# Delta rule layer: the convolution's input is copied from PSUM to SBUF by ScalarE before VectorE reads it

## The chip, the cores and the metric

The kernel runs on one core of a Trainium2 chip. The time is the device time of one execution in microseconds (us); of several runs the median counts.

## What is computed

The reference is two layers of two blocks each. The change is in the first block alone, a gated delta rule over 8 sequences of 512 tokens with 128 channels, 8 key heads and 16 value heads of width 64. Cut to what matters:

```python
mixed = hidden_states @ W_qkv.T                    # 2048 channels: keys, queries, values
y = conv_general_dilated(x, conv_w, ...)           # causal, 4 taps, each channel by itself
mixed = silu(y)
z = hidden_states @ W_z.T
def step(Sst, inp):                                # once per token
    Sst = Sst * exp(g_t)
    kv = einsum('bhkv,bhk->bhv', Sst, k_t)
    delta = (v_t - kv) * b_t
    Sst = Sst + k_t * delta
    o = einsum('bhkv,bhk->bhv', Sst, q_t)
```

Behind it stand an output norm and projection, a mixture of experts, and a second layer (attention beside a state space scan, then experts).

## The kernel before

The program has one instruction stream for each engine, written out in full; engines meet at semaphores that count named steps. The first block (`layer0_delta`) takes the first half of the program. It works on chunks of 64 tokens, 8 for each sequence, 64 in all. Six kinds of work are interleaved by `in_turn`: generators for each engine give a few instructions and yield, and one round over all of them is called a **turn** below. In a turn every engine's stream gets, in this order: a piece of the state recurrence (`state_*`), a step of each of the two solvers T0 and T1 (`solve_*`, which invert a triangular matrix by products L742, copies by ScalarE L823 and additions by VectorE L874), a piece of the projection of tokens still to come (`project_*`), and a piece of the output norm and projection (`output_*`). All engines have the same turns, and each engine works through its stream in order, so an instruction that waits holds up all that stand behind it on its engine.

The projection works on halves of a sequence (256 tokens), 16 in all: for each half 16 blocks of 128 channels (4 of keys, 4 of queries, 8 of values), two blocks to a turn. For a block TensorE multiplies into a PSUM bank (L433, 256 tokens and the 3 before them), and VectorE convolves: one `tensor_scalar` (L599) and three `scalar_tensor_tensor` (L602), each reading the bank at another offset and, from the second on, adding into the destination (`ch_k`, `ch_q` or `ch_v`) in SBUF. When all blocks are done, ScalarE applies silu.

Banks 6 and 7 are **shared**, in strict alternation, by the projection and the output. `into` gives the next of the two and has TensorE wait for the signal that its last reader is done; for a block of the convolution that is the last of its four VectorE instructions, `c{i}0`:

```python
def into(signal):
    n = go.take()
    if go.free[n] is not None:
        pe.wait_ge(*go.free[n])
    go.free[n] = signal
    return go.banks[n]
```

Others that take these banks are the output's two sums of squares for each pair of chunks (L1127, steps n0 and n1, read by ScalarE's L1151), its projection (L1133, read by VectorE's L1176) and the z blocks (L440, read by ScalarE's L515). GpSimd (POOL) makes the squares (L1195) and the scaled outputs (L1200) behind L1127 and its logarithm and exponential on ScalarE (L1151, L1153), and for each chunk the decayed keys, queries and state (L1050, L1051, L1068); all these read and write SBUF alone.

Of the kernel before, what the change touches and what calls it, by code (L numbers as in the profile page):

```python
# [9 lines left out]
ALU = mybir.AluOpType  # L10
ACT = mybir.ActivationFunctionType
AX = mybir.AxisListType
EXP_LN = "natural_log_exp_and_others"

P = 128
# [8 lines left out]
NCHUNK = S // C64  # L24
NM = NB * NCHUNK
HALF = S // 2
NP = NVH // 2
E = 8
F = 512
# [59 lines left out]
class Ctx:  # L89
# [6 lines left out]
    def sb(self, name, shape, dtype=F32):  # L96
        return self.stack.enter_context(self.nc.sbuf_tensor(name, shape, dtype))
# [79 lines left out]
def delta_constants(C, made):  # L177
# [11 lines left out]
    nid64 = w["nid64"] = C.sb("nid64", [P, DK])  # L189
    mask_o = w["mask_o"] = C.sb("mask_o", [P, C64], BF16)  # L190
    mask_a = w["mask_a"] = C.sb("mask_a", [P, C64], BF16)
    wide_o, wide_a = C.sb("wide_o", [P, P]), C.sb("wide_a", [P, P])
    pick = w["pick"] = C.sb("pick", [96, NVH, C64], BF16)
    minus = w["minus"] = C.sb("minus", [96, 2, NP, C64], BF16)
    reset = w["reset"] = C.sb("reset", [96, S])
# [23 lines left out]
    for u in range(2):  # L219
        pool.tensor_scalar(minus[:, u, :, :], id32[0:96, u:NVH:2].unsqueeze(2).to_broadcast([96, NP, C64]), -1.0, None, ALU.mult).then_inc(wave(), 1)  # L220

# [14 lines left out]
class Gates:  # L236
# [4 lines left out]
    ACT = ["ln", "rs", "xn", "a", "b", "ea", "la", "eb", "lb", "beta", "eg", "kf", "cols"]  # L241
# [26 lines left out]
class Channels:  # L268


    PE = [f"x{i}" for i in range(16)] + [f"z{i}" for i in range(4)]
    ACT = [f"z{i}" for i in range(4)] + ["k", "q", "v0", "v1", "sz0", "sz1"]
    DVE = [f"c{i}{j}" for i in range(16) for j in (3, 2, 1, 0)]

    def __init__(self, C):
        sb = C.sb
        self.k = [sb(f"ch_k{i}", [P, NG, HALF]) for i in range(2)]
        self.q = [sb(f"ch_q{i}", [P, NG, HALF]) for i in range(2)]
        self.v = [sb(f"ch_v{i}", [P, NP, HALF]) for i in range(2)]
        self.sz = [sb(f"ch_z{i}", [P, NP, HALF]) for i in range(2)]  # L280
        self.pe = C.steps("ch_matmuls", self.PE)
        self.act = C.steps("ch_activations", self.ACT)
        self.dve = C.steps("ch_convolved", self.DVE)


class Solve:
# [5 lines left out]
    ACT = ["da", "do", "low1", "up2", "low2", "up4", "low4", "up8", "low8", "up16", "low16", "low32"]  # L292
# [94 lines left out]
def project_pe(C, G, X, V, T, go):  # L387
# [3 lines left out]
# [6 lines that stand above are left out]
    for hf in range(2 * NB):  # L397
        b, first = hf // 2, (hf % 2) * HALF
        while go.chained < 4 * hf - 5:
            yield  # L400
        xn = G.xn[b % 2]
        if hf % 2 == 0:
            bank = into(G.act.at(b, "xn"))
# [6 lines left out]
            for name in ("a", "b"):  # L410
                bank = into(G.act.at(b, name))
# [5 lines left out]
            bank = into(G.act.at(b, "cols"))  # L417
# [11 lines left out]
            go.gates = b  # L429
            yield  # L430
        for i, block in enumerate(BLOCKS):
            bank = into(X.dve.at(hf, f"c{i}0"))
            pe.matmul(bank[:, 0:HALF + 3], w["w_qkv"][:, block * P:(block + 1) * P], xn[:, first:first + HALF + 3],  # L433
                      start=True, stop=True).then_inc(X.pe.give(hf, f"x{i}"), 1)
            if i % 2:
                yield
        for i in range(4):
            bank = into(X.act.at(hf, f"z{i}"))
# [10 lines left out]
def project_act(C, G, X, V, T, go):  # L449
    act, w = C.nc.scalar, C.w  # L450
    for hf in range(2 * NB):
        b, i = hf // 2, hf % 2
        while go.chained < 4 * hf - 5:
            yield
        if hf % 2 == 0:
# [4 lines left out]
            bank = go.banks[go.take()]  # L460
# [7 lines left out]
            bank = go.banks[go.take()]  # L468
# [5 lines left out]
            bank = go.banks[go.take()]  # L474
# [20 lines left out]
            bank = go.banks[go.take()]  # L495
# [8 lines left out]
            go.gates = b  # L504
            yield
        for n in range(16):
            go.take()
            if n % 2:
                yield
        for n in range(4):  # L510
            bank = go.banks[go.take()]
# [16 lines left out]
def project_dve(C, G, X, V, T, go):  # L528
    dve, w = C.nc.vector, C.w
    for hf in range(2 * NB):  # L530
        b, i = hf // 2, hf % 2
        while go.chained < 4 * hf - 5:
            yield
        if hf % 2 == 0:
            x = G.x[b % 2]
# [52 lines left out]
            yield  # L588
        cw = w["conv0"]
        for n, block in enumerate(BLOCKS):  # L590
            bank = go.banks[go.take()]
            dst = (X.k[i][:, n, :] if n < NG else X.q[i][:, n - NG, :]) if n < 2 * NG else X.v[i][:, n - 2 * NG, :]
            dve.wait_ge(*X.pe.at(hf, f"x{n}"))
            if n == 0 and hf >= 2:
                dve.wait_ge(*V.pe.at(4 * hf - 5, "x"))
                dve.wait_ge(*V.pool.at(4 * hf - 5, "qd"))
                for t in T:
                    dve.wait_ge(*t.pe.at((4 * hf - 5) // 2, "kt"))
            dve.tensor_scalar(dst, bank[:, 3:3 + HALF], cw[:, block, 3:4], None, ALU.mult).then_inc(X.dve.give(hf, f"c{n}3"), 1)  # L599
            for j in (2, 1, 0):  # L600
                dve.wait_ge(*X.dve.at(hf, f"c{n}{j + 1}"))
                dve.scalar_tensor_tensor(out=dst, in0=bank[:, j:j + HALF], scalar=cw[:, block, j:j + 1], in1=dst,  # L602
                                         op0=ALU.mult, op1=ALU.add).then_inc(X.dve.give(hf, f"c{n}{j}"), 1)
            if n % 2:
                yield
# [627 lines left out]
class Router:  # L1233
    PE = ["rt", "rk"]
    ACT = ["ln", "rs"]
# [495 lines left out]
class TileLine:  # L1731
# [3 lines left out]
    ACT = ["nc", "h0", "h1", "h2", "h3", "t0", "t1", "q0", "q1", "ln", "rs", "g0", "g1", "g2", "g3"]  # L1735
# [1866 lines left out]
```

## Time and profile before

| | |
|---|---|
| median of 3 runs | 4654.08 us (4645.75 to 4654.64) |
| span of the profiled execution, first to last instruction | 4621.9 us |
| median less span | 32.2 us |
| TensorE busy over the span | 3777.9 us, 82% |
| VectorE, ScalarE, GpSimd busy | 2632.5, 1833.3 and 1182.1 us |
| mean granted TensorE clock | 0.912 of full speed |

The profiled execution has no time of its own in the listing beside its span; its 4621.9 us are the stretch that the trace covers, and the 32.2 us to the median lie before the first and behind the last instruction, or are the difference of this execution from the median one. Times in the rows are counted from the span's start. The stage of the change ends at about 2362 us; the rest of the program doesn't touch what is changed. PE is TensorE, DVE is VectorE, ACT is ScalarE.

### The profile page before, as it was taken

The numbers are of one execution on the slowest core, as the hardware profiler recorded it, in microseconds if no ns is written. First come the engines' busy times: TensorE is split into PE (matmuls) and PEld (weight loads), VectorE is DVE, ScalarE is ACT, GpSimd is POOL, SyncE is SP. The second block draws the span as 40 slices with busy tenths as digits, with TensorE's granted clock in tenths as the row PEclk, the third lists the DMA queues.
The fourth block names the chain that finished last, engine by engine and source line by source line (L and its number), as shares of the span: only waits on it lengthen the run. The fifth ranks groups of instructions, "written<-read, shape, count | busy, mean of one in ns | idle before, by whom it ended". The sixth has DMA issues, their size and how long they took to land. (4 is left out here: it accounts for less than half of the span.)

```text
span 4621.9 us, 133260 instructions
## 1 busy us (share of the span) xinstructions
PE 3777.9 (82%) x60410; PEld 2904.4 (63%) x60410; DVE 2632.5 (57%) x4402; ACT 1833.3 (40%) x2937; POOL 1182.1 (26%) x1148
## 2 busy tenths in 40 slices
PE   5888989889898898988989999915777887777855
PEld 4877878778687787877878888812333433433424
DVE  5355454544545445454335555544877888888743
ACT  2333333333333333323336666613444454444422
POOL 2131421314213142231345555361000000000063
PEclk9999999999999999999989999957898889898878
DMA  6341000000000000000044444321212222222214
GB/s 198 134 142 41 24 25 11 24 23 26 17 10 21 7 16 18 8 19 7 15 142 161 154 152 155 102 56 42 60 47 51 61 56 51 56 60 53 57 33 132
DMA packets 206516, 284.72 MB, mean 62 GB/s; under 512 B 86712, under 2 KB 148416, under 8 KB 199808
## 3 DMA queue, kind: packets, MB, share of 16 engines
q1 hardware_dynamic: 136160, 111.25, 9.4%
q0 software_dynamic: 24016, 107.80, 7.1%
q10 hardware_dynamic: 45776, 57.15, 3.7%
q8 instruction: 476, 7.80, 0.7%
q14 instruction: 88, 0.72, 0.1%
HBM read 215.59 MB, written 72.61 MB: 62 GB/s over the span
## 5 line engine op out<-in xcount | busy, mean ns | idle before, releaser
L874 DVE TENSOR_TENSOR sd_z<-psum,sd_z 128x512 f32<-128x512 f32 x320 | 219.0, 689 | 415.5 <-PE psum L742 415.0
L2784 PE MATMUL psum<-ss_h,ident 128*128 128x512 f32 x512 | 297.2, 710 | 24.1 <-DVE ss_h L2899 23.6
L2893 DVE TENSOR_TENSOR_SCAN ss_h<-ss_da,ss_h 128x1024 f32<-128x1024 f32 x128 | 294.1, 2298 | 3.5 <-ACT ss_da L2833 3.0
L921 POOL TENSOR_TENSOR sd_z<-id,s_up 128x512 f32<-128x512 f32 x64 | 81.3, 1270 | 812.8 <-DVE s_up L880 812.2
L2541 POOL TENSOR_TENSOR at_qs<-at_q,slot_of 128x512 f32<-128x512 f32 x32 | 45.6, 1435 | 951.3 <-ACT at_q L2411 706.8
L1802 PE MATMUL psum<-e_h,e_mid_w 128*128 128x256 f32 x1248 | 283.8, 381 | 1.0 <-ACT e_h L1846 1.0
L1802 PEld LDWEIGHTS psum<-e_h,e_mid_w 128*128 128x128 f32 x1248 | 238.4, 191 | 34.0 <-ACT e_h L1846 1.6
L742 PE MATMUL psum<-sd_z,s_do 64*64 64x64 f32 x6144 | 223.8, 227 | 30.1 <-ACT s_do L823 28.6
L742 PEld LDWEIGHTS psum<-sd_z,s_do 64*64 64x64 f32 x6144 | 205.9, 142 | 64.8 <-issue 33.8
L742 PE MATMUL psum<-s_low,s_up 64*64 64x64 f32 x6144 | 225.1, 225 | 24.9 <-DVE sd_z L874 22.3
L2454 ACT ACTIVATE x_tok<-psum 128x512 f32<-128x512 f32 x320 | 165.2, 603 | 192.4 <-PE psum L2379 192.2
L1195 POOL TENSOR_TENSOR out_sq<-st_h 128x512 f32<-128x512 f32 x64 | 66.4, 1038 | 620.2 <-PE psum L1127 372.5
L742 PEld LDWEIGHTS psum<-s_low,s_up 64*64 64x64 f32 x6144 | 205.1, 140 | 30.5 <-DVE sd_z L874 24.4
L823 ACT ACTIVATE s_low<-psum 128x512 f32<-128x512 f32 x192 | 114.6, 597 | 270.3 <-PE psum L771 176.7
L2514 DVE TENSOR_REDUCE at_mx<-psum 128x4 f32<-128x1536 f32 (+3 forms) x88 | 184.3, 2094 | 49.2 <-PE psum L2355 48.6
L602 DVE SCALAR_TENSOR_TENSOR ch_v<-psum,conv,ch_v 128x256 f32<-128x256 f32 x384 | 185.8, 484 | 13.7
L2784 PEld LDWEIGHTS psum<-ss_h,ident 128*128 128x128 f32 x512 | 103.0, 224 | 140.1 <-issue 87.6
L823 ACT ACTIVATE s_do<-psum 128x512 f32<-128x512 f32 x192 | 114.6, 597 | 191.2 <-PE psum L742 191.2
L433 PE MATMUL psum<-g_xn,w_qkv 128*128 128x259 f32 x512 | 160.6, 431 | 34.4 <-DVE ch_k L602 18.2
L2352 PE MATMUL psum<-at_k,at_qs 32*128 32x384 f32 (+3 forms) x1024 | 110.8, 532 | 85.2 <-DVE at_mx L2514 63.7
L742 PE MATMUL psum<-s_do,s_da 64*64 64x64 f32 x4096 | 152.4, 226 | 32.3 <-DVE sd_z L874 32.3
L823 ACT ACTIVATE s_da<-psum 128x512 f32<-128x512 f32 x128 | 76.4, 597 | 252.6 <-PE psum L742 252.5
(472 smaller groups left out, 9883.7 us busy)
## 6 DMA issues: line engine op xcount, KB each, us to landing
ss_rows<-bc_scratch SPq DMA_DIRECT2D x128, 512.0 KB, 4.9
answered<-ce_zeros ACTq DMA_DIRECT2D x19, 1024.0 KB
routed<-ce_zeros ACTq DMA_DIRECT2D x16, 1024.0 KB, 9.1
st_eg<-gate_scratch SPq DMA_DIRECT2D x128, 128.0 KB, 5.2
table_mid<-in_t_mid ACTq DMA_DIRECT2D x4, 1536.0 KB
m_w<-in_m_w ACTq DMA_DIRECT2D x16, 256.0 KB, 7.7
table_down<-in_t_down ACTq DMA_DIRECT2D x1, 2560.0 KB
g_x<-in_x SPq DMA_DIRECT2D x8, 256.0 KB, 6.0
```

The costliest lines, as they stand in the source:

```text
L433: pe.matmul(bank[:, 0:HALF + 3], w["w_qkv"][:, block * P:(block + 1) * P], xn[:, first:first + HALF + 3], start=True, stop=True).then_inc( ...
L602: dve.scalar_tensor_tensor(out=dst, in0=bank[:, j:j + HALF], scalar=cw[:, block, j:j + 1], in1=dst, op0=ALU.mult, op1=ALU.add).then_inc(X. ...
L742: t = pe.matmul(bank[half(u), p * C64:(p + 1) * C64], left[half(u), p, :], right[half(u), p, :], start=True, stop=True)
L823: act.activation(dst[:, :, :].rearrange("p a t -> p (a t)"), bank[:, :], ACT.Copy).then_inc(T.act.give(r, name), 1)
L874: dve.tensor_tensor(d.z[:, :, :], bank[:, :].rearrange("p (a t) -> p a t", a=NP), d.z[:, :, :], ALU.add).then_inc(T.dve.give(r, name), 1)
L921: pool.tensor_tensor(D[m % 3].z[:, :, :], w["id64"][:, :].unsqueeze(1).to_broadcast([P, NP, C64]), T.up[:, :, :], ALU.subtract).then_inc(T ...
L1802: t = pe.matmul(part[m], X.mid(j, m), X.h1[:, j, :], start=(j == 0), stop=(j == FB - 1))
L2352: pe.matmul(banks[:, r, s * nk:(s + 1) * nk], q[rows, n + s, :], k[rows, 0:nk], start=(s == 0), stop=False, skip_group_check=True)
L2454: act.activation(A.weights(t, n, r)[:, :], C.bank[r][:, :], ACT.Exp).then_inc(A.act.give(t, f"e{n}{r}"), 1)
L2514: dve.tensor_reduce(A.mx[:, n:n + slots, 0:P:32].rearrange("p s r -> p r s"), C.psum[:, 0:4, 0:slots * nk].rearrange("p r (s k) -> p r s k ...
L2784: t = pe.matmul((b5, b6)[m][:, :], w["ident"][:, :], Z.h_of(b, n)[:, m, :], start=False, stop=(n == DS - 1), skip_group_check=True)
L2893: dve.tensor_tensor_scan(flat, flat2(Z.da[n % 2][:, :, :]), flat, 0.0, ALU.mult, ALU.add).then_inc(Z.dve.give(b, f"s{n}"), 1)
```

## The change

ScalarE copies each block's bank to one of two new SBUF buffers (`ch_raw`, 128 x 259, used in alternation), and VectorE's four instructions read the buffer. TensorE's bank is now given back by ScalarE's copy (step `r{i}`). The copy of block n waits for the matmul and for the end of the convolution of block n - 2. To make room, two constant masks use a part of the tile `s0`, at the program's start.

```diff
+RAWS = 2
-    wide_o, wide_a = C.sb("wide_o", [P, P]), C.sb("wide_a", [P, P])
+    wide_o, wide_a = C.s0[:, 0, :], C.s0[:, 1, :]
...
-    ACT = [f"z{i}" for i in range(4)] + ["k", "q", "v0", "v1", "sz0", "sz1"]
+    ACT = [f"r{i}" for i in range(16)] + [f"z{i}" for i in range(4)] + ["k", "q", "v0", "v1", "sz0", "sz1"]
...
+        self.raw = [sb(f"ch_raw{i}", [P, 3 + HALF]) for i in range(RAWS)]
...
-            bank = into(X.dve.at(hf, f"c{i}0"))
+            bank = into(X.act.at(hf, f"r{i}"))
...
         for n in range(16):
-            go.take()
+            bank = go.banks[go.take()]
+            act.wait_ge(*X.pe.at(hf, f"x{n}"))
+            if n >= RAWS:
+                act.wait_ge(*X.dve.at(hf, f"c{n - RAWS}0"))
+            elif hf:
+                act.wait_ge(*X.dve.at(hf - 1, f"c{16 + n - RAWS}0"))
+            act.activation(X.raw[n % RAWS][:, :], bank[:, 0:3 + HALF], ACT.Copy).then_inc(X.act.give(hf, f"r{n}"), 1)
...
-            bank = go.banks[go.take()]
+            go.take()
+            raw = X.raw[n % RAWS]
...
-            dve.wait_ge(*X.pe.at(hf, f"x{n}"))
+            dve.wait_ge(*X.act.at(hf, f"r{n}"))
...
-            dve.tensor_scalar(dst, bank[:, 3:3 + HALF], cw[:, block, 3:4], None, ALU.mult).then_inc(X.dve.give(hf, f"c{n}3"), 1)
+            dve.tensor_scalar(dst, raw[:, 3:3 + HALF], cw[:, block, 3:4], None, ALU.mult).then_inc(X.dve.give(hf, f"c{n}3"), 1)
...
-                dve.scalar_tensor_tensor(out=dst, in0=bank[:, j:j + HALF], scalar=cw[:, block, j:j + 1], in1=dst,
+                dve.scalar_tensor_tensor(out=dst, in0=raw[:, j:j + HALF], scalar=cw[:, block, j:j + 1], in1=dst,
```

No instruction moves on TensorE, GpSimd or SyncE. ScalarE gets 256 new ones, two at the end of each projection turn. On ScalarE, at the fifth projection turn of the first half of the second sequence, before the change (`s0` and `s1` in the waits are the solvers T0 and T1, `out` the output):

```order
L823 ACTIVATE s_up<-psum 128x512 [waits s0_matmuls]
L823 ACTIVATE s_low<-psum 128x512 [waits s0_matmuls]
L823 ACTIVATE s_up<-psum 128x512 [waits s1_matmuls,s1_pool]
L823 ACTIVATE s_low<-psum 128x512 [waits s1_matmuls]
L1151 ACTIVATE out_rstd<-psum,eps_rms 128x512 [waits out_pool,out_matmuls]
L1153 ACTIVATE out_rstd<-out_rstd 128x512 [waits out_activations]
```

and at the same place after it:

```order
L832 ACTIVATE s_up<-psum 128x512 [waits s0_matmuls]
L832 ACTIVATE s_low<-psum 128x512 [waits s0_matmuls]
L832 ACTIVATE s_up<-psum 128x512 [waits s1_matmuls,s1_pool]
L832 ACTIVATE s_low<-psum 128x512 [waits s1_matmuls]
L515 ACTIVATE ch_raw<-psum 128x259 [waits ch_convolved,ch_matmuls] x2
L1160 ACTIVATE out_rstd<-psum,eps_rms 128x512 [waits out_pool,out_matmuls]
L1162 ACTIVATE out_rstd<-out_rstd 128x512 [waits out_activations]
```

The two copies stand between the solvers' copies and the output's logarithm; all other lines are 2 to 9 numbers further down. On VectorE, at a projection turn of the second half of the first sequence, before:

```order
L874 TENSOR_TENSOR sd_z<-psum,sd_z 128x512 [waits s1_matmuls,s1_pool]
L599 TENSOR_SCALAR ch_v<-psum,conv 128x256 [waits ch_matmuls]
L602 SCALAR_TENSOR_TENSOR ch_v<-psum,conv,ch_v 128x256 [waits ch_convolved] x3
L599 TENSOR_SCALAR ch_v<-psum,conv 128x256 [waits ch_matmuls]
L602 SCALAR_TENSOR_TENSOR ch_v<-psum,conv,ch_v 128x256 [waits ch_convolved] x3
L874 TENSOR_TENSOR sd_z<-psum,sd_z 128x512 [waits s0_matmuls,s0_vectors]
```

and after:

```order
L883 TENSOR_TENSOR sd_z<-psum,sd_z 128x512 [waits s1_matmuls,s1_pool]
L608 TENSOR_SCALAR ch_v<-ch_raw,conv 128x256 [waits ch_activations]
L611 SCALAR_TENSOR_TENSOR ch_v<-ch_raw,conv,ch_v 128x256 [waits ch_convolved] x3
L608 TENSOR_SCALAR ch_v<-ch_raw,conv 128x256 [waits ch_activations]
L611 SCALAR_TENSOR_TENSOR ch_v<-ch_raw,conv,ch_v 128x256 [waits ch_convolved] x3
L883 TENSOR_TENSOR sd_z<-psum,sd_z 128x512 [waits s0_matmuls,s0_vectors]
```

Nothing moves here: the instructions have the same neighbours, but read `ch_raw` where they read PSUM, and wait for ScalarE where they waited for TensorE.

## Rows read from the trace of the kernel before

**Rows 1.** Window of one sequence: PE, PEld, DVE, ACT, POOL busy us (count); clock

```profile
865.00:1154.00 289.00, 254.62 (x6199) 223.96 (x6198) 142.67 (x277) 100.36 (x160) 76.64 (x71) 0.94 0.08 22
```

**Rows 2.** Line L602: durations min/median/max; who waited for it (us, times)

```profile
L602 DVE SCALAR_TENSOR_TENSOR ch_v<-psum,conv,ch_v x384: 483/484/486, 53.3 to 2165.8; 128x256 f32<-128x256 f32 x192
...
  PE psum L1127: 47.0, 28
...
  PE psum L433: 33.5, 36
...
  PE psum L1133: 24.7, 14
```

**Rows 3.** Timeline, a sequence's first half, fifth projection turn: start, us, what, idle before

```profile
898.02 1.14 PE L433 MATMUL psum<-g_xn,w_qkv 128*128 128x259 f32 x4
900.86 1.12 PE L1127 MATMUL psum<-out_sq,head_ones 128*128 128x512 f32 x2 [1.70 <-DVE ch_v L602]
...
898.76 0.48 DVE L599 TENSOR_SCALAR ch_v<-psum,conv 128x256 f32<-128x256 f32 x1 [1.88 <-PE psum L433]
...
903.18 0.69 DVE L874 TENSOR_TENSOR sd_z<-psum,sd_z 128x512 f32<-128x512 f32 x1 [0.43 <-PE psum L742]
...
902.07 1.04 POOL L1195 TENSOR_TENSOR out_sq<-st_h 128x512 f32<-128x512 f32 x1 [15.94 <-PE psum L1127]
```

**Rows 4.** Timeline, a turn whose additions TensorE waits for

```profile
894.00 1.15 PE L742 MATMUL psum<-s_do,s_da 64*64 64x64 f32 x32 [2.24 <-DVE sd_z L874]
```

**Rows 5.** Timeline, the second sum of squares (PE, ACT) and GpSimd's chain behind it

```profile
909.71 1.13 PE L1127 MATMUL psum<-out_sq,head_ones 128*128 128x512 f32 x2 [1.70 <-DVE ch_v L602]
...
913.71 1.15 PE L742 MATMUL psum<-s_do,s_da 64*64 64x64 f32 x32
...
910.87 0.69 ACT L1151 ACTIVATE out_rstd<-psum,eps_rms 128x512 f32<-128x512 f32 x1 [3.29 <-PE psum L1127]
...
912.30 1.27 POOL L1200 TENSOR_TENSOR st_h<-st_h,out_rstd 128x512 f32<-128x512 f32 x1 [7.58 <-ACT out_rstd L1153]
...
918.21 1.27 POOL L1051 TENSOR_TENSOR st_qd<-ch_q,st_eg 128x512 f32<-128x512 f32 x1
```

**Rows 6.** Timeline, second half of the same sequence: TensorE behind eight blocks

```profile
958.35 2.07 PE L1127 MATMUL psum<-out_sq,head_ones 128*128 128x512 f32 x2 [2.04 <-DVE ch_k L602]
...
971.88 1.15 PE L742 MATMUL psum<-s_do,s_da 64*64 64x64 f32 x32
...
981.29 1.97 PE L742 MATMUL psum<-s_low,s_up 64*64 64x64 f32 x32 [2.24 <-DVE sd_z L874]
...
971.14 0.69 DVE L874 TENSOR_TENSOR sd_z<-psum,sd_z 128x512 f32<-128x512 f32 x1 [0.42 <-PE psum L742]
```

**Rows 7.** Forms on VectorE and ScalarE: busy us, mean ns | idle before

```profile
L2737 DVE SCALAR_TENSOR_TENSOR ss_xc<-ss_raw,conv,ss_xc 128x512 f32<-128x512 f32 x48 | 35.8, 746 | 1.1
L1642 DVE TENSOR_SCALAR s<-s,ce_sums 128x512 f32<-128x512 f32 x12 | 5.3, 480 | 0.1
L2734 DVE TENSOR_SCALAR ss_xc<-ss_raw,conv,conv_b 128x512 f32<-128x512 f32 x16 | 8.6, 539 | 4.6 <-ACT ss_raw L2689 4.6
L2433 ACT ACTIVATE at_oc<-psum 128x128 f32<-128x128 f32 x32 | 8.8, 276 | 155.4 <-PE psum L2316 155.4
L823 ACT ACTIVATE s_da<-psum 128x512 f32<-128x512 f32 x128 | 76.4, 597 | 252.6 <-PE psum L742 252.5
```

**Rows 8.** Timeline, VectorE beside GpSimd, both reading SBUF alone

```profile
259.28 4.58 DVE L573 TENSOR_TENSOR g_b<-g_b,g_tb 96x512 f32<-96x512 f32 x1
...
259.82 1.27 POOL L1050 TENSOR_TENSOR st_kg<-ch_k,st_eg 128x512 f32<-128x512 f32 x1
...
262.26 1.04 POOL L1068 TENSOR_TENSOR st_scd<-st_s,g_cols 128x512 f32<-128x512 f32 x1
```

**Rows 9.** The same pair of engines, short instructions on VectorE

```profile
490.70 1.15 DVE L1394 TENSOR_TENSOR m_order<-m_order,down 128x32 f32<-128x32 f32 x1
...
490.50 1.29 POOL L1051 TENSOR_TENSOR st_qd<-ch_q,st_eg 128x512 f32<-128x512 f32 x1
```

## The prediction

> **What bounds the kernel now.** I first read the windows. In one sequence's stretch of 289 us, eight times repeated up to 2362 us, TensorE is busy 254.6 us, 88%, VectorE 49%, ScalarE 35%, GpSimd 27% [rows 1]. So TensorE's stream is nearly the time of the stage, and what counts is who makes it wait. Line L602's list of waiters shows it: TensorE waited 47.0 + 33.5 + 24.7 = 105.2 us, 78 times, for a convolution to give back a shared bank [rows 2]. That is 13.2 us a sequence, 2.3% of the whole, and the most that the early return of the bank can give directly.
>
> Then the timeline, for what stands behind such a wait. In the fifth projection turn TensorE issues the two blocks at 898.02 and then waits 1.70 us for the first block's convolution until L1127 starts at 900.86. VectorE convolves from 898.76 and is through shortly before 903.18, when the solver's addition L874 starts after an idle 0.43 us [rows 3]. So both engines are near their limit here: the addition stands behind both blocks in VectorE's order, and TensorE needs it for its next but one product. In other turns VectorE is already the later one: TensorE waits 2.24 us for an addition behind a convolution at 894.00 [rows 4] and again at 981.29 [rows 6].
>
> **The change part by part.**
>
> *ScalarE's copy.* ACT copies of 512 columns from PSUM take 597 ns, of 128 columns 276 ns [rows 7]: 0.836 ns a column, so 276 + 131 x 0.836 = 386 ns for 259. 256 of them are 99 us on an engine that is 35% busy; they fit. A bank comes free about 0.4 us after its matmul where it took 1.96 us of VectorE (four instructions of about 0.49 us). But VectorE starts about 0.43 us later (copy and one more semaphore) in each turn in which it waited for the block.
>
> *VectorE's reads.* L602 takes 484 ns at 256 columns from PSUM [rows 2]. From SBUF the same form takes 746 ns at 512 [rows 7]; less 256 columns at 1.04 ns that is 480 ns. No gain. L599 takes 0.48 us [rows 3]; from SBUF `tensor_scalar` takes 480 to 539 ns at 512 columns [rows 7], two columns a cycle, so less 256 at 0.52 ns: 347 to 406 ns; I take 380, 0.1 us less a block, 0.2 us a turn. Net, a turn's convolution ends 0.43 - 0.2 = 0.23 us later if VectorE waited for its block, and 0.2 us sooner if it didn't. The Trainium skill (VectorE: DVE Perf Modes, the section on the TRN2 errata) gives a fixed 58 cycles for a source in SBUF and 120 for PSUM. By that each of the 1024 instructions would gain 65 ns, a turn's convolution 0.5 us, and in the some six turns of a sequence in which TensorE waits for an addition that would be 3 us, in all 24 us off the sum below: 4645 us. Rows 2 and 7 show nothing of it for the 768 of L602, so the sum leaves it out and I give it under 1 in 20.
>
> *A port between VectorE and GpSimd.* Before, one of the two sources of L602 is in PSUM; after, both are in SBUF. What that does beside GpSimd stands in rows 8: L573, both sources in SBUF, 512 columns as L874, which takes 0.69 us [rows 3], started at 259.28 and took 4.58, until GpSimd's three products (259.82 to 263.30) were over. With small instructions the pattern is milder: L1394, 32 columns, started at 490.70 during L1051 and took 1.15 us, that is to this one product's end [rows 9], and it got in ahead of the next. L602 from PSUM never took over 486 ns [rows 2], though GpSimd's chain 912.30 to 919.48 [rows 5] ran across a whole turn of it. The Trainium skill (SBUF — State Buffer, SBUF: two separate sides) has it as a rule: a VectorE instruction with two SBUF inputs and a GpSimd one that reads SBUF exclude each other for the whole instruction. Rows 8 agree. No row shows an L602-like instruction against GpSimd; the bounds are 0 and the whole of GpSimd's work beside it, 1.04 to 1.27 us for each of its instructions. I take the pattern of rows 9, one product each time, since the convolution's instructions come one behind another.
>
> *Where these meet.* I put the rows of one sequence forward, engine by engine.
>
> First half. Up to the fifth turn two turns of the kind of [rows 4] come 0.24 us later each: +0.5. Fifth turn: L1127 starts 1.1 us earlier, but its follower on GpSimd, L1195, started at 902.07 only 0.1 us behind it [rows 3]; now that falls into the convolution, and L1200 follows on the exponential. Two exclusions, 2.3 us; the addition comes at 905.4 for 903.18, TensorE's product behind the next addition is 1.0 us late. Sixth turn: L1127 waits no more, so the logarithm, the exponential and L1200 start 1.7 us earlier against the convolution, and L1200 heads a chain of six products without a gap (912.30 to 919.48) [rows 5]. It now begins before the second block is through. Three instructions of L602 each let one product past: the two additions end at 916.3 and TensorE's 913.71 product starts 2.6 us late. Then the seventh turn finds less of the chain, and L1133's wait in the eighth (1.8 us) is saved: +0.9 us at the half's end.
>
> Second half. TensorE waits for banks through four blocks and L1127 starts at 958.35 [rows 6]; with copies it starts at about 955, and the next blocks' matmuls and the second L1127 some 6 us earlier than before. But VectorE has all six blocks to convolve without a pause, 6 x 1.86 = 11.2 us from 951.6, and 0.8 of another instruction, plus two L1195 and L1200 (3.3 us), plus four of the chain's products (4.5 us): 971.3 for the addition that started at 971.14 [rows 6]. The 6 us are gone. Then +0.35 in a turn of the kind of rows 4, -1 at the second L1133, -0.15: -0.6 us for the half.
>
> Sum of a sequence: +0.9 - 0.6 = +0.3 us. The waits of 3 and 7 us for additions that TensorE gets instead have a price in its clock: behind the 2.24 us at 981.29 a group that takes 1.15 us elsewhere took 1.97, the granted clock was at half, 1.2 of 2.4 GHz, for about 3 us [rows 6], but the same had happened at 958.35 (2.07 us for L1127, 1.13 elsewhere), so one more such stretch, 1.6 us. Together 1.9 us a sequence, times 8 is 15 us. The two masks in `s0` cost nothing: they are made before anything waits for them. Against the profiled span: 4621.9 + 15 = 4637, and with 32.2 us around it 4669. The span and the median of the runs differ by that constant alone.
>
> **The rivals.**
>
> *The port hardly matters, and the bank's early return is the gain.* Without exclusions my steps give, in the first half, -1.4 (fifth turn), -0.5 (sixth), -1.5 (L1133), +0.5: -2.9; in the second, -7.4 at 971.14 (the six blocks end at 963.7) and -1.0 at L1133: -8.4. -11.3 us a sequence of the 13.2 at most, 90 in all: 4564, and 4609 where half of it is lost to exclusions or VectorE's later start. For it speaks that no row shows the very instruction excluded, and that a convolution that ends sooner meets less of GpSimd. Against it: rows 8, that GpSimd is busy 27% of the time [rows 1], which for 16 turns of 3.9 us would be 17 us a sequence if it fell blindly (my steps place some 16), and that the instructions of GpSimd which follow L1127 are moved into the convolution. It decides if exclusions cost under 5 us a sequence.
>
> *GpSimd wins every time.* By the pattern of L573 [rows 8] VectorE would stand until the whole chain of six is over: in the sixth turn to 918.7, the additions end at 920, and TensorE is 6.3 us late for my 2.6; in the second half 1.3 us more. 5 us a sequence, 40 in all on top of the sum: 4709. It decides when GpSimd's next product is ahead of a waiting VectorE.
>
> *ScalarE holds up TensorE.* A copy waits for the convolution two blocks back, and the solver's copies and the exponentials stand behind it. Where VectorE is 3 us late, ScalarE is too. Within my steps it costs nothing; if the solvers' copies came 1 us later in 4 turns a sequence, it would be 32 us more, 4701.
>
> **How the numbers follow.** 0.2% of 4654 is 9 us, about what a measurement of this kernel can tell from no change. The first case, exclusions and gain near each other, has 0.45, from 4645 to 4700, and 4669 is its middle. The gain that stays has 0.27, 4564 to 4645. The two costlier ones have 0.25 (0.17 and 0.08), 4690 to 4735, and 0.03 is left for none of them. The range of 4605 to 4720 leaves out the far half of the gain and the end of the last. Of the first case 0.17 lies within 9 us, and 0.05 of the others: same 0.22; faster 0.28, slower 0.50.
>
> **What would show it.** In the profile of the changed kernel TensorE's waits for the convolution are gone from L1127, L433 and L1133, few for ScalarE's copy replace them, and waits for L874 (the addition) grow by as much: that is right if they grow by about 100 us. L602's successor has a median of 480 to 485 ns, but a maximum of 1.5 us and more, and a mean of 550 to 650; if its maximum stays under 500 ns, the port doesn't matter and the first rival holds. GpSimd's products get a maximum of about 1.7 us if the two alternate, and stay at 1.27 if GpSimd always wins. The copies take 386 ns, `tensor_scalar` 350 to 400. I'd be wrong above all if the exclusions fall elsewhere than my steps put them, since every shift moves both engines.

## The result, and the profile after

The changed kernel takes 4632.03 us (median of 6 runs, 4623.32 to 4642.88), the kernel before, run beside it, 4653.68 us (6 runs, 4642.08 to 4666.5). The ratio is 0.9948 with a 95% interval of 0.9934 to 0.9962: 22 us faster. A second group of runs gave 0.9957 (0.9945 to 0.9970). The forecast was 15 us slower. The result lies inside its range, but on the other side of zero.

| | before | after |
|---|---|---|
| median, this group | 4653.68 us | 4632.03 us |
| profiled execution: time; span | not recorded; 4621.9 us | 4632.81; 4631.0 us |
| TensorE waits for the convolution's bank | 106.6 us, 80 times | none |
| TensorE waits for ScalarE's copy | | 18.2 us, 21 times |
| TensorE waits for the addition `sd_z` | 54.7 us, 31 times | 121.9 us, 58 times |

The profiled execution after has 1.8 us around its span, and so has every other run for which both are recorded (1.7 to 1.9). The 32.2 us that the prediction put around the span of before are therefore for the most part the difference between that execution and the median run: by 1.8 us around its span it took some 4624 us (an estimate). So the two spans can't be compared with each other. The groups' ratios can, and so can the waits, which repeat better: in a second profile of the change they are 124.5 us for the addition (121.9 in the first) and 18.4 for the copy (18.2).

Line numbers have moved: L433 is L435, L599 is L608, L602 is L611, L742 is L751, L874 is L883, L1127 is L1136, L1195 and L1200 are L1204 and L1209. ScalarE's copy is L515. The lists of line L515 (with who waited for it), L608, L611 and L1209 (durations are minimum/median/maximum in ns), of the changed kernel:

```profile
L515 ACT ACTIVATE ch_raw<-psum x256: 387/387/432, 37.2 to 2158.1; 128x259 f32<-128x259 f32 x128
...
  PE psum L435: 12.5, 13
...
  PE psum L1136: 5.1, 7
...
  PE psum L442: 0.6, 1
L608 DVE TENSOR_SCALAR ch_v<-ch_raw,conv x128: 341/349/1248, 55.5 to 2161.0; 128x256 f32<-128x256 f32 x128
L611 DVE SCALAR_TENSOR_TENSOR ch_q<-ch_raw,conv,ch_q x192: 483/485/1452, 48.6 to 2131.8; 128x256 f32<-128x256 f32 x192
L1209 POOL TENSOR_TENSOR st_h<-st_h,out_rstd x64: 1257/1274/1473, 185.6 to 2354.8; 128x512 f32<-128x512 f32 x64
```

The 78 waits of [rows 2] are gone. The medians of VectorE's two instructions are 349 ns (476 before) and 485 ns (484 before): no gain in the second. But its maximum is now 1452 ns (486 before), and GpSimd's product L1209 of 1274 ns can take 1473 (1287 before). That is what is called an **exclusion** below: an instruction of one of the two engines is stretched while one of the other runs. What it adds up to is read from the mean durations, of the changed kernel in the stretch 0 to 2370 us:

```profile
L611 DVE SCALAR_TENSOR_TENSOR ch_v<-ch_raw,conv,ch_v 128x256 f32<-128x256 f32 x384 | 209.7, 546 | 13.7
L611 DVE SCALAR_TENSOR_TENSOR ch_q<-ch_raw,conv,ch_q 128x256 f32<-128x256 f32 x192 | 111.8, 583 | 6.8
L611 DVE SCALAR_TENSOR_TENSOR ch_k<-ch_raw,conv,ch_k 128x256 f32<-128x256 f32 x192 | 109.6, 571 | 6.8
L608 DVE TENSOR_SCALAR ch_v<-ch_raw,conv 128x256 f32<-128x256 f32 x128 | 48.8, 381 | 95.3 <-ACT ch_raw L515 95.2
L608 DVE TENSOR_SCALAR ch_k<-ch_raw,conv 128x256 f32<-128x256 f32 x64 | 28.7, 448 | 41.6 <-ACT ch_raw L515 41.6
```

L611 has 384 x 61 + 192 x 98 + 192 x 86 ns = 59 us over its median, L608 128 x 32 + 64 x 99 ns = 10 us over 349. That is 70 us, 8.8 us a sequence. In the trace's single records 80 instructions, 10 a sequence, lie 0.6 us or more over their median. Together they are 67.5 us over it, 0.84 us each in the mean; 0.88 is the most frequent, and 0.97 the most for L611.

What it does to the sum is read best in the sixth turn, that of [rows 5]. The timeline of the changed kernel there (start, duration, then what it waited for in brackets):

```profile
913.52 1.13 PE L1136 MATMUL psum<-out_sq,head_ones 128*128 128x512 f32 x2
...
920.32 1.15 PE L751 MATMUL psum<-s_do,s_da 64*64 64x64 f32 x32 [2.73 <-DVE sd_z L883]
...
913.89 1.52 DVE L611 SCALAR_TENSOR_TENSOR ch_v<-ch_raw,conv,ch_v 128x256 f32<-128x256 f32 x3
...
915.71 3.35 DVE L611 SCALAR_TENSOR_TENSOR ch_v<-ch_raw,conv,ch_v 128x256 f32<-128x256 f32 x3
...
918.99 1.27 DVE L883 TENSOR_TENSOR sd_z<-psum,sd_z 128x512 f32<-128x512 f32 x2
...
916.11 1.27 POOL L1209 TENSOR_TENSOR st_h<-st_h,out_rstd 128x512 f32<-128x512 f32 x1 [7.42 <-ACT out_rstd L1162]
917.34 1.45 POOL L1059 TENSOR_TENSOR st_kg<-ch_k,st_eg 128x512 f32<-128x512 f32 x1
918.74 1.45 POOL L1060 TENSOR_TENSOR st_qd<-ch_q,st_eg 128x512 f32<-128x512 f32 x1
```

L1136 waits for nothing (1.70 us before). The first block's three instructions take 1.52 us, the second block's 3.35, since GpSimd's chain has begun in its midst; TensorE, no more held at L1136, now waits 2.73 us at L751 for the addition behind that block. The shift of this product against the sequence's start is 1.4 us (920.32 less 913.71, less the 5.2 us by which the sequence begins later in this trace); the prediction had 2.6.

The second half, that of [rows 6]:

```profile
960.74 1.12 PE L1136 MATMUL psum<-out_sq,head_ones 128*128 128x512 f32 x2 [0.78 <-ACT ch_raw L515]
...
966.96 1.12 PE L1136 MATMUL psum<-out_sq,head_ones 128*128 128x512 f32 x2
...
975.20 1.97 PE L751 MATMUL psum<-s_do,s_da 64*64 64x64 f32 x32 [5.11 <-DVE sd_z L883]
...
963.97 2.46 DVE L611 SCALAR_TENSOR_TENSOR ch_k<-ch_raw,conv,ch_k 128x256 f32<-128x256 f32 x3
...
970.38 4.17 DVE L611 SCALAR_TENSOR_TENSOR ch_q<-ch_raw,conv,ch_q 128x256 f32<-128x256 f32 x3
974.47 0.68 DVE L883 TENSOR_TENSOR sd_z<-psum,sd_z 128x512 f32<-128x512 f32 x1
```

TensorE runs ahead, as forecast, and then stands 5.11 us for an addition that starts 1.9 us earlier than before (974.47 less 5.2 against 971.14), where the prediction had it equal. The exclusions among these blocks are 0.94 (the 2.46 less 1.52), 2.65 (4.17 less 1.52) and 0.66 us (a group of 2.18 at 958.03, not shown). With 0.85 us on another VectorE instruction between the blocks (L1651, the L1642 of before: 1.72 for 0.87) that is 5.1 us, for the 7.8 us counted.

### The profile page after: what moved, and what is told of

Same layout as the page of the kernel before. It is cut to its first block and busy times, and to the rows that moved or that the text cites. A ratio compares the mean times of both kernels' runs of the same rounds, so it can differ in the third digit from the quotient of the medians.

```text
span 4631.0 us, 133770 instructions
## 1 busy us (share of the span) xinstructions
PE 3790.0 (82%) x60410; PEld 2916.7 (63%) x60410; DVE 2668.9 (58%) x4402; ACT 1926.5 (42%) x3193; POOL 1189.7 (26%) x1148
## 5 line engine op out<-in xcount | busy, mean ns | idle before, releaser
L883 DVE TENSOR_TENSOR sd_z<-psum,sd_z 128x512 f32<-128x512 f32 x320 | 217.5, 688 | 387.0 <-PE psum L751 387.0
L930 POOL TENSOR_TENSOR sd_z<-id,s_up 128x512 f32<-128x512 f32 x64 | 81.5, 1273 | 844.8 <-DVE s_up L889 844.2
L751 PE MATMUL psum<-sd_z,s_do 64*64 64x64 f32 x6144 | 225.1, 228 | 31.0 <-ACT s_do L832 29.2
L751 PE MATMUL psum<-s_low,s_up 64*64 64x64 f32 x6144 | 220.3, 222 | 36.7 <-DVE sd_z L883 35.4
L751 PEld LDWEIGHTS psum<-sd_z,s_do 64*64 64x64 f32 x6144 | 207.0, 143 | 63.1 <-issue 31.0
L751 PE MATMUL psum<-s_do,s_da 64*64 64x64 f32 x4096 | 162.8, 232 | 91.1 <-DVE sd_z L883 86.5
L751 PEld LDWEIGHTS psum<-s_low,s_up 64*64 64x64 f32 x6144 | 200.6, 137 | 42.3 <-DVE sd_z L883 38.4
L1204 POOL TENSOR_TENSOR out_sq<-st_h 128x512 f32<-128x512 f32 x64 | 67.1, 1048 | 589.2 <-PE psum L1136 339.6
L611 DVE SCALAR_TENSOR_TENSOR ch_v<-ch_raw,conv,ch_v 128x256 f32<-128x256 f32 x384 | 209.7, 546 | 13.7
L751 PEld LDWEIGHTS psum<-s_do,s_da 64*64 64x64 f32 x4096 | 144.9, 145 | 102.3 <-DVE sd_z L883 91.5
L1886 DVE TENSOR_SCALAR e_pre<-psum,e_down_w 128x256 f32<-128x256 f32 x156 | 77.2, 535 | 166.0 <-ACT e_t L1860 140.4
```

The source lines that it names most:

```text
L611: dve.scalar_tensor_tensor(out=dst, in0=raw[:, j:j + HALF], scalar=cw[:, block, j:j + 1], in1=dst, op0=ALU.mult, op1=ALU.add).then_inc(X.d ...
L751: t = pe.matmul(bank[half(u), p * C64:(p + 1) * C64], left[half(u), p, :], right[half(u), p, :], start=True, stop=True)
L883: dve.tensor_tensor(d.z[:, :, :], bank[:, :].rearrange("p (a t) -> p a t", a=NP), d.z[:, :, :], ALU.add).then_inc(T.dve.give(r, name), 1)
```

## The experiments

Every ratio is to the kernel before in the same group of runs, with its 95% interval. Groups ran on different chips and differ by up to 42 us in the median of before (4618.86 to 4660.49), so microseconds are compared inside one group, or as ratios times 4654.

**Late return.** The copies and SBUF reads of the change, but the bank is given back where it was before:

```
-            bank = into(X.act.at(hf, f"r{i}"))
+            bank = into(X.dve.at(hf, f"c{i}0"))
```

> Everything as in the change, but TensorE waits for the convolution's last step before it takes the block's bank again, as before the change, though nobody reads the bank after ScalarE's copy. Theory A (the gain of the change is the early return; reading from SBUF and the exclusions with GpSimd only cost): TensorE's waits for the convolution are back, not at 106 us but at 106 + some 78 x 0.3 us for the copy ahead of it + about half of the 70 us of exclusions, so the time is 30 to 60 us over before: 4685 to 4715 us, ratio to before 1.006 to 1.013. Theory B (the change won its 22 us because VectorE has less work, the tensor_scalar from SBUF taking 349 ns for 480, and the bank's return mattered little): no slower than before, 4630 to 4654 us.

Measured 1.0152 (1.0128 to 1.0175), 70 us slower, a little beyond the forecast's end. TensorE waits 53.8 + 52.3 + 30.0 + 1.3 = 137.4 us for the convolution and 62.5 us for the addition:

```profile
  PE psum L435: 53.8, 48
  PE psum L1136: 52.3, 28
...
  PE psum L1142: 30.0, 14
```

So the change is two effects of opposite sign. The early return is worth 0.9948/1.0152 = 0.980, 94 us (89 with the second group's 0.9957); what VectorE's reading from the copy costs without it is 70 us. The rival (quicker reads as the gain) is refuted. The exclusions in this run's records are 42 us, for 70 in the change: part of them comes only with the early return, and the 94 us are what is left after paying for those.

**Copies that nobody needs.** ScalarE copies 128x259 from the weights to the two buffers; the rest is the kernel before:

```
+            act.wait_ge(*X.pe.at(hf, f"x{n}"))
+            ...
+            act.activation(X.raw[n % RAWS][:, :], w["w_qkv"][:, 0:3 + HALF], ACT.Copy).then_inc(X.act.give(hf, f"r{n}"), 1)
```

> The kernel before, with 256 copies added on ScalarE that nothing needs: 128x259 fp32, from the projection's weights in SBUF to two unused buffers, each waiting for the same matmul as the change's copy and standing at the same place of ScalarE's order. VectorE convolves from PSUM and gives the bank back, as before. It prices ScalarE's 100 us and its waits alone. Theory A: ScalarE has the room, within 0.2% of before (4645 to 4663 us); TensorE's waits for ScalarE grow by less than 5 us. Theory C (ScalarE's evictions and exponentials come late behind the copies, and the change would have won more without it): slower than before by 10 to 30 us, and TensorE's waits with ScalarE as the releaser grow by as much.

Measured 1.0001 (0.9988 to 1.0015). 107 us of extra ScalarE time (419 ns each) cost nothing, and TensorE's waits are those of [rows 2] to the tenth: 47.0, 33.5, 24.7. Theory C falls. One part of the prediction's third rival is not tested by this kernel: here a copy waits only for the copy two blocks back, in the change for the convolution two blocks back, and ScalarE waited 58.7 us for that there (45 times). The trace of the change shows what came of it. TensorE's waits for the solver's copies behind it are 29.2 us for 28.6 before, and the 18.2 us for the copy itself are what it adds to TensorE's waits.

**The later start alone.** As the last, and VectorE's first step waits for the unneeded copy too:

```
             dve.wait_ge(*X.pe.at(hf, f"x{n}"))
+            dve.wait_ge(*X.act.at(hf, f"r{n}"))
```

> As the run with 256 unneeded copies on ScalarE, and now VectorE's first step on each block also waits for the unneeded copy. It still convolves from PSUM, the bank comes back at the convolution's end, nothing is excluded by GpSimd: this prices the later start of VectorE (copy and one more semaphore, 0.4 us) alone. The late return with the copies read cost 1.0152 of before, 70 us. Theory A (the two costs are of like size: some 38 us of exclusions were in that run's records on VectorE and 0.1 us a block was won back by the tensor_scalar): 35 to 50 us of it is the later start (78 waits for banks and 31 for additions by 0.3 to 0.4 us each), ratio 1.008 to 1.011. Rival D (exclusions are nearly all of it): ratio at most 1.004.

Measured 1.0116 (1.0097 to 1.0136): 54 us, slightly over the forecast. The waits for the convolution are 130.3 us (+24), for the addition 67.5 us (+13). So the later start alone costs about as much as three quarters of the late return's 70 us. The unneeded copy takes 32 ns longer than that of the change, so this price is a little high.

**Without GpSimd's reads.** Three kernels in which GpSimd writes a constant in place of its products, the first on the kernel before, the second on the change, the third on the late return (the products are left out of all three):

```
-        pool.tensor_tensor(by_key(V.kg[m % 2]), of_key(X.k[i]), by_key(eg), ALU.mult).then_inc(V.pool.give(m, "kg"), 1)
+        pool.memset(V.kg[m % 2][:, :, :], 0.01).then_inc(V.pool.give(m, "kg"), 1)
...
-            pool.tensor_tensor(h, h, O.rstd[i][:, :, :], ALU.mult).then_inc(O.pool.give(n, f"hn{i}"), 1)
+            pool.memset(h, 0.01).then_inc(O.pool.give(n, f"hn{i}"), 1)
```

> The kernel before with GpSimd's products of keys, queries, state, heads and squares (L1050, L1051, L1068, L1195, L1200) replaced by a memset of the same tile: GpSimd reads nothing in SBUF beside the convolution, and the products are left out, so the output is not the reference's. It is the base for the two other kernels without these products. GpSimd's chains get shorter, so it should be faster than before by up to 1%; the ratio itself tells nothing, its PE waits for the convolution should be near the 106 us of before.

> The change, with GpSimd's products left out and replaced by memsets in the same way (output not the reference's). Theory A (exclusions with GpSimd cost the change some 50 to 70 us): L611 has a mean of 484 to 490 ns and a maximum under 600 for 546 to 583 and 1452, TensorE's waits for the addition fall from 122 to 70 to 90 us, and against the base without products the ratio is 0.978 to 0.987 where with them it was 0.995. Rival (the exclusions lie beside other work, the waits for the addition come from the later start): ratio to that base 0.991 to 0.997.

> The change with the bank given back only at the convolution's end, and with GpSimd's products left out and replaced by memsets (output not the reference's). With the products this late return cost 1.0152 of before. Theory A: without exclusions 1.003 to 1.009 of the base without products are left, the later start less the quicker tensor_scalar. Rival (exclusions matter little): 1.012 to 1.017.

Measured: 0.9936 (0.9919 to 0.9953), 0.9737 (0.9722 to 0.9751) and 1.0015 (1.0003 to 1.0026). Against the first, the change is 0.9737/0.9936 = 0.9800 (roughly 0.978 to 0.982), 93 us faster, and the late return 1.0080, 37 us slower; both lie in theory A's forecast. So what these products cost through exclusions is 0.9948 - 0.9800 in the change, that is 69 us (give or take 13), and 1.0152 - 1.0080, 33 us, in the late return. Of the late return's 70 us then 33 are exclusions and 54 the later start. The -17 that are left fit the quicker `tensor_scalar`, but are only this remainder; no run shows them by themselves. Without the products the early return is worth 0.9737/1.0015 = 0.972, 129 us, where with them it was 94. The lists of lines L611 and L883 in the changed kernel without the products:

```profile
L611 DVE SCALAR_TENSOR_TENSOR ch_v<-ch_raw,conv,ch_v x384: 483/485/486, 55.9 to 2067.5; 128x256 f32<-128x256 f32 x192
...
  PE psum L751: 75.9, 53
```

L611 on the values stays within 486 ns, and the wait for the addition is 75.9 us for 121.9. On the keys its maximum is 1317 ns, over the 600 forecast, since at the program's start GpSimd still has products of the gates beside it. All in all L611 lies 1.4 us over its median for 59 in the change, but L608 still 9.3 for 10.6. So this kernel takes away 59 of the 70 us in the records, and the price of the change falls by 69. GpSimd's memsets are also shorter than its products (530 ns for 1274). The first kernel has them too: its waits for the bank (106.9 us) and the addition (53.7 us) are those of before, while TensorE's waits for GpSimd's decayed keys (L1050) halve, 17.5 us for 35.2. In the second kernel they are 17.4 us, so TensorE's own waits for GpSimd have no part in its 93 us; that the shorter memsets help in another way isn't ruled out.

**Tap 3 on ScalarE, from the bank.** On the kernel before: ScalarE multiplies by the fourth tap instead of VectorE. No copy, no early return:

```
+            act.activation(dst, bank[:, 3:3 + HALF], ACT.Copy, scale=w["conv0"][:, block, 3:4]).then_inc(X.act.give(hf, f"r{n}"), 1)
...
-            dve.tensor_scalar(dst, bank[:, 3:3 + HALF], cw[:, block, 3:4], None, ALU.mult).then_inc(X.dve.give(hf, f"c{n}3"), 1)
```

> The kernel before, with the convolution's first product (tap 3) given to ScalarE: an activation Copy with the tap's column as scale, from the bank straight into the keys, queries or values. VectorE does only the three scalar_tensor_tensor, from PSUM. No SBUF copy, no early return (the bank is free after VectorE's last step), one SBUF source only, so no exclusion with GpSimd. A turn's convolution takes VectorE 2.9 us for 3.9. Theory A: TensorE's waits for the convolution fall from 106 to some 60 to 75 us (a turn of two blocks ends about 0.55 us sooner), its waits for the addition L874 stay at or under 55 us, L602 keeps a mean of 484 ns: 4600 to 4630 us. Rival: what VectorE saves lies beside other work and the bank comes back nearly as late as before (0.4 + 1.45 us for 1.93): 4645 to 4660 us. If it is under the 4632 us of the change, the early return is not the best use of ScalarE.

Measured 0.9844 (0.9823 to 0.9864), 4549.74 us beside 4625.04. The forecast of 4600 to 4630, made from 4654, is 0.988 to 0.995: the gain is larger than either theory had it. The waits for the convolution fell only to 43.3 + 23.6 + 18.4 + 0.7 = 86.0 us, less than forecast, those for the addition to 34.8 us. Its groups on the two lines of the convolution:

```profile
L605 DVE SCALAR_TENSOR_TENSOR ch_v<-psum,conv,ch_v 128x256 f32<-128x256 f32 x384 | 179.9, 482 | 113.3 <-ACT ch_v L515 104.1
L515 ACT ACTIVATE ch_v<-psum,conv 128x256 f32<-128x256 f32 x128 | 58.6, 473 | 31.2 <-PE psum L433 29.7
```

**Tap 3 on ScalarE, and the copy.** On the change, with the same activation ahead of the copy:

> The change, with ScalarE also doing tap 3 from the bank into the keys, queries or values before it copies the bank to the small buffer. VectorE does three scalar_tensor_tensor from SBUF, the bank is free about 0.8 us after its matmul. Two SBUF sources, so the exclusions stay. Theory A (VectorE's lateness, 122 us of waits for the addition L883, is what eats the change's gain): without 0.35 to 0.45 us a block on VectorE these waits fall to 60 to 80 us, against it each of VectorE's first steps starts 0.4 us later, ScalarE has 200 us more than before: 4590 to 4620 us. Rival C (ScalarE, 35% busy before, becomes the one that is late: its evictions and exponentials stand behind two copies a block): 4632 to 4670 us, TensorE waits for ScalarE over 60 us.

Measured 0.9781 (0.9762 to 0.9801), 4520.85 us; and once more in the last group:

> Tap 3 by ScalarE and all blocks copied, once more, so that it stands beside the partial one and the change in the same group of runs: 0.976 to 0.980 of before, as the first time.

0.9787 (0.9774 to 0.9799), 4521.92 us. It is the fastest of the kernels that compute everything, 104 and 97 us under before, and beyond the first forecast (4590 to 4620 of 4654, 0.986 to 0.993), though VectorE's reads are still stretched (557 and 616 ns for values and keys). TensorE's wait for the addition is 57.2 us for the change's 121.9 (60 to 80 forecast). The time, though, is about the product of the two steps, 0.9844 x 0.9948 = 0.9793: the copy gains no clearly larger share with tap 3 moved than without. The group of the values, and the list of waiters for the addition's line:

```profile
L613 DVE SCALAR_TENSOR_TENSOR ch_v<-ch_raw,conv,ch_v 128x256 f32<-128x256 f32 x384 | 208.3, 557 | 119.0 <-ACT ch_raw L522 109.9
```

```profile
  PE psum L753: 57.2, 48
```

**Copies only in the turns without exclusions.** Sixteen blocks in each half, two a turn:

```
+def copied(hf, n):
+    return n >= 6 if hf % 2 else n >= 14
...
+            bank = into(X.act.at(hf, f"r{i}") if copied(hf, i) else X.dve.at(hf, f"c{i}0"))
...
+            raw = X.raw[n % RAWS] if copied(hf, n) else bank
```

> The change in part of the turns only. In the trace of the change the exclusions with GpSimd fall into the turns 4, 5, 6, 8, 9 and 10 of a sequence's 16 (8.4 of 9.0 us a sequence; a turn is two blocks), while turns 7, 12, 14 and 15 had 4.4 of the 13.3 us of bank waits before and have none. So ScalarE copies only blocks 14 and 15 of a first half and 6 to 15 of a second (turns 7 and 11 to 15); in the others VectorE reads the bank and gives it back, as before the change. Theory A (each turn's saving and price stand where the traces show them): the bank waits of 71 us stay, 35 us are saved, nearly no exclusion: L611 with ch_raw has a mean under 500 ns, ratio to before 0.992 to 0.995, that is as good as the whole change with 96 copies instead of 256. Rival (the turns hang together: an earlier start in one turn moves GpSimd's products of the next into a convolution, or what is saved comes back as a wait for the addition): 0.996 to 1.001.

> ScalarE does tap 3 of all blocks straight from the bank, and copies the bank only for turns 7 and 11 to 15 of a sequence; in the other turns VectorE's three steps read the bank. Theory A: the 0.984 of tap 3 alone, and on top the 25 to 35 us of the early return in turns with no exclusion: 0.976 to 0.980. Rival (turns hang together, as above): 0.981 to 0.985. Beside tap 3 with all blocks copied (0.978 when first run) this tells if the exclusions in turns 4 to 10 still cost what the early return gives there.

> The changed kernel once more, timed in the same group as the others: 0.993 to 0.997 of before, as the first time (0.9948). If it is under 0.992 or over 0.998 the sum of the two halves of the effect (early return 94 us, the reads' price 70 us) is not stable from group to group.

Measured 0.9957 (0.9944 to 0.9970), 0.9846 (0.9833 to 0.9860) and 0.9957 (0.9945 to 0.9970). With 96 copies instead of 256 the first is as fast as the whole change, just over its forecast's end. Its exclusions are nearly gone (4.5 us), its bank waits stand at 73.0 us (71 forecast), and 63.3 us for the addition. Its lines' lists (L615 is L611, L755 is L751):

```profile
L615 DVE SCALAR_TENSOR_TENSOR ch_v<-ch_raw,conv,ch_v x240: 483/485/486, 64.9 to 2145.4; 128x256 f32<-128x256 f32 x120
...
  PE psum L1140: 47.0, 28
...
  PE psum L441: 26.0, 29
  PE psum L755: 63.3, 37
```

So in the other 80 turns' 160 copies the change pays about as much as it gains (to some 8 us, by the two intervals). With tap 3 moved that isn't so: 0.9846 for the partial one against 0.9787 for all blocks. There the early return is worth 0.006 more than its exclusions in just those turns; that this is because VectorE is less late is argued from the 57 us of waits for the addition, not shown by itself. The forecast for the partial kernel with tap 3 was wrong, its rival's size right: it gained nothing over tap 3 alone (0.9844).

## Why the prediction was wrong

**The mechanism held.** The copies take 387 ns (386 forecast), `tensor_scalar` 349 (347 to 406), L611 485 (480 to 484). The waits at L1127, L433 and L1133 went, and waits for the addition took their place: +67 us, about 100 forecast. L611's maximum is 1452 ns (1.5 us), its mean 546 to 583 (550 to 650), GpSimd's maximum 1473 (about 1.7 us; L1060 has 1509). The second half came where the steps put it before the exclusions: the second L1136 is 7.1 us earlier against the sequence's start, some 6 forecast.

**The step that failed is the price of the exclusions**, "three instructions of L602 each let one product past", "plus two L1195 and L1200 (3.3 us), plus four of the chain's products (4.5 us)", "my steps place some 16" us a sequence. The exclusions that it names one by one are 12, worth about 14 us. The records show 8.8 us, with 10 exclusions of 0.6 us or more. One costs VectorE 0.84 us in the mean, not the 1.04 to 1.27 of the GpSimd instruction that it lets past. The pattern of [rows 9] and the count were about right, the price of one was too high. In the sixth turn two products were let past for the three forecast, and the second half had 5 us for 7.8. In the sum the exclusions stood for the way from -11.3 to +0.3, that is 11.6 us a sequence or 93 us; the kernels without GpSimd's products put them at 69 us, 8.6 a sequence. The prediction also let the gain win only if they cost under 5; by its own -11.3 the change loses only beyond 11.

**The second failed term is the clock**, 1.6 us a sequence, 13 us. The long wait does have its slow stretch (groups of 1.97, 1.92 and 1.60 us from 975.20), but the one of before at 958.35 is gone (L1136 takes 1.12 us where L1127 took 2.07), and that of [rows 6] at 981.29 is still there (1.98 us at 986.69, 5.4 us later). So this sequence has two such stretches, as before, not one more. In the whole stage, groups of L742 or L751 with 32 matmuls that take over 1.7 us number 53 before, 54 and 48 in the two profiles after. No run shows this cost.

**The first rival's figure held**: -90 us without exclusions, measured -93. So -93 + 69 = -24 us for the 22 measured (the 69 are themselves taken from those 22, so this is no second test), where the prediction's own terms gave -90 + 93 + 13 = +15 (rounded). The agreement of 90 with 93 is in part luck, since the 93 have two parts. TensorE executes 49574 or 49575 matmuls up to the stage's end in each kernel below; without GpSimd's products the change takes 66 us off its waits (303 to 237, all rows of the waits in the stage summed) and 24 off its busy time:

```profile
0.00:2360.00 2360.00, 2046.10 (x49575) 0.95 0.13 39
...
0.00:2271.00 2271.00, 2021.96 (x49574) 0.95 0.14 41
```

My steps had all of it as waits. For the change itself the waits up to the stage's end fall from 318 to 305 us in the first profile and 310 in the second. The other 10 us or so of the 22 would have to lie in TensorE's busy time, and there the two profiles of the same kernel disagree (2052 and 2023 us, for 2047 before). So how much the clock gave in this case stays open.

**The frame of the sum.** The prediction took the 32.2 us between span and median for a constant. The other runs have 1.8 us there, so the 4669 stands on a span and a median of different executions; the ratio forecast isn't touched by it.

**The other rivals.** That GpSimd wins every time is refuted for L611: the two alternate. (For `tensor_scalar` see the last section.) ScalarE's work costs nothing by itself (copies that nobody needs: 1.0001), and its lateness behind VectorE costs TensorE the 18.2 us of waits for the copy and 0.6 us at the solver's.

On the rules that were weighed. L611 and L602 differ by 1 ns in their median, so nothing of a cheaper source in SBUF shows for this instruction. Beside that stands the Trainium skill (VectorE: DVE Perf Modes, the section on the TRN2 errata) with 58 cycles for SBUF and 120 for PSUM; its 4645 us would have been nearer than 4669, for a reason the trace doesn't bear out. GpSimd's chain beside VectorE has a period of 1.40 us (917.34 to 918.74), with one VectorE instruction let in each time; alone they take 1.27 and 0.485, 1.76 in sum. The Trainium skill (SBUF — State Buffer, SBUF: two separate sides) has them exclude each other for the whole instruction; the alternation agrees, the 0.36 us by which the period is shorter than the sum does not.

## What to carry to other kernels

Giving a bank back early shifts the wait to whatever the slow engine does next, here from 107 to 18 us at the banks and from 55 to 122 at the addition. Taking an instruction off that engine was worth three times as much here (tap 3: 0.984) as taking its input out of the bank (0.995), and the two added up (0.978). Where an edit makes an engine read two SBUF operands beside GpSimd, count the meetings, but price one by how far such an instruction's mean lies over its median in a trace, not by the whole of GpSimd's instruction. And measure opposed effects apart, by kernels with one of them each: here 94 us and 70 us hid behind a difference of 22. Their sizes depend on each other (the early return is worth 129 us without the exclusions that it brings), so say which of them was in place.

## What the runs showed of the hardware

A microsecond of wait taken from TensorE gave back more than itself in these pairs. With tap 3 on ScalarE its waits up to the stage's end fell by 39 us (314 to 275) against the kernel with unneeded copies, whose time is that of before, but the stage by 72 us: as many matmuls were busy 35 us less, at a mean granted clock of 0.95 for 0.93. The windows of the two, the unneeded copies first:

```profile
0.00:2369.00 2369.00, 2045.45 (x49574) 0.93 0.13 39
...
0.00:2297.00 2297.00, 2010.58 (x49575) 0.95 0.14 41
```

The late return went the other way, 44 us more wait and 29 us more busy. As the two profiles of the change show, 29 us of busy time can also differ from one execution to the next of one kernel, so the size for a single pair is uncertain. The medians bear it out: 75 us between the two kernels (12 and 5 runs), with a mean granted clock of 0.903 to 0.913 over the unneeded copies' executions and 0.913 to 0.919 over those with tap 3 moved. That it is the clock which shortens the busy time is read from these two columns together, not tested.

The two instructions of the convolution differ in what holds them up. Where GpSimd writes memsets, `scalar_tensor_tensor` stays at its 485 ns beside them, but `tensor_scalar` from SBUF doesn't. In the change without GpSimd's products 87 of the first ran beside a memset, none over 486 ns; of the second 16 did, and 15 of them took over 400 ns, 349 otherwise. The longest started at 90.06 beside the solver's product L930 and ended at 92.77, past five memsets in a row (90.24 to 92.62):

```profile
90.06 2.71 DVE L608 TENSOR_SCALAR ch_k<-ch_raw,conv 128x256 f32<-128x256 f32 x1
...
90.24 0.52 POOL L1059 MEMSET st_kg<- 128x512 f32 x1
90.70 0.52 POOL L1060 MEMSET st_qd<- 128x512 f32 x1
...
92.10 0.52 POOL L1060 MEMSET st_qd<- 128x512 f32 x1
```

ScalarE took 387 ns for 128x259 from PSUM, and 419 ns for the same from SBUF; with a column of scales, 128x256 from PSUM, 473 ns.
